# Moving the rotation of three query chunks and the bias rows from VectorE to GpSimd, from batch 1 on

## What is computed

```python
q = hidden_states @ w_q.T            # 16 heads of 32
k, v = jnp.split(hidden_states @ w_kv.T, 2, axis=-1)
def apply_rotary(t, pos, scale):
    return t * jnp.cos(pos) * scale + rotate_half(t) * jnp.sin(pos) * scale
q = apply_rotary(q, pos, xscale)
k = apply_rotary(k, pos, 1.0 / xscale)
attn = softmax(where(causal, -inf, q @ k.T))
out = (attn @ v) @ w_proj.T + b_proj
x = x + out + ffn(xn)
```

## Time and profile before

| | us |
|---|---|
| three runs: median (lowest, highest) | 1730.41 (1730.21, 1731.7) |
| the profiled execution | 1730.02 |
| its span, first instruction to last | 1728.2 |
| busy in the span: TensorE / VectorE / ScalarE / GpSimd | 1620.8 / 1205.5 / 1073.1 / 821.0 |

### The profile page before, as it was taken

The page is one execution under the profiler, slowest core; times in us unless marked ns, Lnnn a source line. Parts: engine busy times, 40 slices in busy tenths (PEclk is TensorE's granted clock), DMA queues, the critical chain, the costliest instruction groups (busy, mean ns, idle before and its releaser), DMA issues.

```text
span 1728.2 us, 40624 instructions
## 1 busy us (share of the span) xinstructions
PE 1620.8 (94%) x10811; PEld 1388.4 (80%) x10811; DVE 1205.5 (70%) x3669; ACT 1073.1 (62%) x2799; POOL 821.0 (48%) x669
## 2 busy tenths in 40 slices
PE   5887789999999999999999999899999999999999
PEld 5775667777777877777777777799999999999987
DVE  7779987777868777778687777355555555555567
ACT  3355565666757756757577577366666666666642
POOL 0213002434524524435344344277777877778760
PEclk9899899999999999999999999999999999999999
DMA  7953823434434334344344344599999999989794
GB/s 280 387 166 102 134 63 99 142 115 145 140 96 151 124 126 153 113 137 136 116 138 133 105 151 141 117 183 188 182 195 187 189 187 198 201 172 162 137 260 184
DMA packets 193091, 273.72 MB, mean 158 GB/s; under 512 B 37400, under 2 KB 133791, under 8 KB 190820
## 3 DMA queue, kind: packets, MB, share of 16 engines
q0 software_dynamic: 60352, 92.59, 24.8%
q1 hardware_dynamic: 77572, 113.01, 23.2%
q10 hardware_dynamic: 54944, 65.52, 12.8%
HBM read 121.83 MB, written 129.67 MB: 146 GB/s over the span
## 4 chain that ended last, share of the span: by engine, by line
PE 58%; DVE 18%; issue 10%; DMA 5%; POOL 4%; ACT 3%; DVEq 1%; SPq 1%; ACTq 0%; POOLq 0%
PE e_psH L1710 10%; PE e_psY L1721 10%; DVE m_sc L1088 5%; POOL sums L1675 4%; PE m_psO L1339 4%; PE m_psU L64 3%; PE m_psS L1292 3%; PE m_psT L1317 3%; PE m_psY L64 3%; PE m_psU L66 3%; PE m_psU L65 3%; DVE m_sc L1098 3%; PE m_psY L65 3%; PE m_psY L66 3%; PE e_psX L1695 3%
## 5 line engine op out<-in xcount | busy, mean ns | idle before, releaser
L1675 POOL DMA_INDIRECT sums<-e_y,e_where x287 | 445.9, 1554 | 153.4 <-issue 96.5
L856 POOL DMA_INDIRECT slot_rows<-m_row,slots x256 | 266.1, 1039 | 470.4 <-ACT m_sc L934 436.8
L934 ACT ACTIVATE m_sc<-m_sc,m_low 128x512 f32<-128x512 f32 (+3 forms) x512 | 283.7, 556 | 161.5 <-DVE m_low L1088 160.1
L1710 PE MATMUL e_psH<-e_xt,e_w_of 128*128 128x128 f32 x2296 | 305.1, 276 | 3.3 <-ACT e_xt L1570 3.3
L1721 PE MATMUL e_psY<-e_w,e_ht 128*128 x1148 | 295.7, 380 | 1.5 <-ACT e_ht L1581 1.5
L1088 DVE CUSTOM_DVE_ANT_0 m_sc<-m_psS,cst 128x512 f32<-128x512 f32 (+3 forms) x512 | 229.4, 485 | 83.1 <-PE m_psS L1292 82.5
L1710 PEld LDWEIGHTS e_psH<-e_xt,e_w_of 128*128 128x128 f32 x2296 | 280.5, 193 | 3.7 <-ACT e_xt L1570 3.5
L1576 ACT ACTIVATE e_w_of<-e_w 128x512 f32 x287 | 180.9, 630 | 118.1 <-issue 116.1
L1721 PEld LDWEIGHTS e_psY<-e_w,e_ht 128*128 128x128 f32 x1148 | 196.2, 191 | 17.2 <-issue 2.5
L1292 PE MATMUL m_psS<-m_ks,m_qs 96*128 96x256 f32 (+2 forms) x512 | 160.2, 372 | 52.1 <-DVE m_low L1088 45.1
L1631 DVE TENSOR_SCALAR e_where<-e_row,e_shifts 128x1 uint32<-128x1 uint32 x287 | 61.5, 214 | 196.5 <-DMA sums<-e_y,e_where 178.2
(11 more groups left out here) (233 smaller groups left out, 3228.2 us busy)
## 6 DMA issues: line engine op xcount, KB each, us to landing
e_row<-slot_rows ACTq DMA_DIRECT2D x287, 144.5 KB, 3.7
m_qs<-m_qhi SPq DMA_DIRECT2D x256, 64.0 KB
e_w<-in_w SPq DMA_DIRECT2D x256, 64.0 KB
f_xt<-in_x SPq DMA_DIRECT2D x8, 1024.0 KB, 11.4
m_qs<-m_qlo SPq DMA_DIRECT2D x128, 64.0 KB
m_res<-in_x SPq DMA_DIRECT2D x8, 1024.0 KB, 5.8
sums<-empty POOLq DMA_DIRECT2D x32, 256.0 KB
partial<-m_res ACTq DMA_DIRECT2D x16, 512.0 KB
```

The lines of the kernel that those rows point to most:

```text
L856: pool.indirect_dma_start(out=xs, out_offset=bass.IndirectOffsetOnAxis(ap=slots_sb[:, g, k:k + 1], axis=0), in_=row[g % 2][:, :], in_offse ...
L934: nc.scalar.activation(cols, cols, ACT.Exp, bias=low[:, h % 2, i:i + 1], scale=-1.0, accum_out=total[:, h % 2, i:i + 1]).then_inc(exp_done, 1)
L1675: pool.indirect_dma_start(out=both_sums, out_offset=bass.IndirectOffsetOnAxis(ap=where[u % NY][:, 0:1], axis=0), in_=y[u % NY][:, :], in_o ...
L1710: mm = pe.matmul(psH[u % 2][:, k * P:(k + 1) * P], w1_of[u % 2][:, c * INTER + k * P:c * INTER + (k + 1) * P], xt[u % 2][:, c * P:(c + 1) ...
```

## The change

From batch 1 on, GpSimd makes the two products and the sum of the chunks 1 to 3 and adds the four bias rows; batch 0, chunk 0 and the keys stay as they are. VectorE keeps the shuffle. The GpSimd work stands in program order among its scatters: a chunk's turn after the last scatter that waits for no more than the first row of exponentials of step 1, 5 or 9, and the bias rows after the last one that waits for no more than all rows of step 5. The core of the diff:

```diff
+            def turn_queries(b, n):
+                cos, sin = tables["q"]
+                k = QK_AT[f"q{n}"]
+                pool.wait_ge(rot_step, at(b, 3 * NQK, 3 * k + 1))
+                pool.sem_inc(pool_passed, 1)
+                nc.gpsimd.tensor_tensor(rot[:, :], rot[:, :], sin, ALU.mult).then_inc(rot_step, 1)
+                nc.gpsimd.tensor_tensor(q[:, :], q[:, :], cos, ALU.mult).then_inc(rot_step, 1)
+                pool.wait_ge(rot_step, at(b, 3 * NQK, 3 * k + 3))
+                nc.gpsimd.tensor_tensor(q[:, :], q[:, :], rot[:, :], ALU.add).then_inc(rotated, 1)
+
+            def add_bias(b):
+                pool.wait_ge(res_in, b * 16 + 16)
+                pool.wait_ge(bp_in, 16)
+                pool.sem_inc(pool_passed, 1)
+                for i in range(TB):
+                    nc.gpsimd.tensor_tensor(res[:, i, :], res[:, i, :], bp[:, :], ALU.add).then_inc(res_made, 1)
+
+            def beside(done, due):
+
+                for b in range(1, B):
+                    for n in range(1, KC):
+                        if done <= b * NH * TB + (q_slot(n) + 1) * TB + 1 < due:
+                            turn_queries(b, n)
+                        if n == 2 and done <= b * NH * TB + (q_slot(n) + 2) * TB < due:
+                            add_bias(b)
+
+            def paced(g, k):
+                return NH * TB + (g * TOPK + k) * PACE // (2 * TOPK)
+
             def scatter(g, k):
+                beside(paced(g, k - 1) if g or k else 0, paced(g, k))
...
-                if 0 in parts:
+                if 0 in parts or not parts:
...
                     nc.vector.stream_shuffle(r_, x_, [(i + HD // 2) % HD for i in range(HD)]).then_inc(rot_step, 1)
+                if 0 in parts:
...
-                        rotate(b, f"q{Q_AT[s - 1]}", (0,))
+                        rotate(b, f"q{Q_AT[s - 1]}", (0,) if first else ())
...
-                    if s - 2 in Q_AT:
+                    if first and s - 2 in Q_AT:
                         rotate(b, f"q{Q_AT[s - 2]}", (1,))
...
-                    if 5 <= s < 5 + TB:
+                    if first and 5 <= s < 5 + TB:
                         add_bias(b, s - 5)
```

More of the change, by code:

```diff
@@ L878, in pool_program @@
                 fill(g)
+            beside(paced(G - 1, TOPK - 1), B * NH * TB + NH * TB)
             for u in range(2):
```

## The result

The changed kernel took **1779.68 us** (median of 4 runs, 1778.05 to 1784.06) against 1731.06 us before: ratio 1.0287, 95% interval 1.0273 to 1.0301. It is 49 us slower, where 16 us were forecast. Its profiled execution has a span of 1776.1 us, 47.9 more than before.

What follows compares the result with a forecast made beforehand. The last-ending chain was 58% TensorE and 18% VectorE, with VectorE's extra work on the path in slots 2, 6 and 10. 1730.0 - 18.8 gained + 35.7 lost = 1746.9 us; forecast 1734 to 1762 (0.64), range 1718 to 1763.

Steps and rivals of the forecast that it cites:

- the term of slot 6: Slot 6: GpSimd's four bias rows meet VectorE's square, subtractions and scale; three hits taken, 2.6 us a batch lost.
- the high end: Slots 1, 5, 9 and 6 at their largest losses, 2.55 + 1.1 + 1.4 + 3.4 = 8.45 us a batch; 1770 us.
- Slot 1: Slot 1: GpSimd's second product and sum run beside VectorE's scale; two hits, 1.7 us a batch lost.
- Slots 5 and 9: Slots 5 and 9: the turn's hits mostly covered by TensorE; 0.4 us a batch lost in each.
- The gain: Slots 1, 2, 6, 7 and 10: VectorE work removed from the path; 2.68 us a batch, 18.8 over seven.
- more cannot go: Slots 2 and 10: savings stop at 0.34 and 0.35 us, as the 0.84 us wait for ScalarE comes back.
- the row that I chose: Batch 0 trace: the square beside a GpSimd operation took 0.43 us, so no hit in slot 6; sum stays at 1747.
- Its 1753: Slot 6: by the skill's port rule the square is held up too, a fourth hit; sum 1753 us.
- GpSimd costs nothing: Rival 1: GpSimd's operations fall beside mask operations and in VectorE's waits; 1711 us at best; chance 0.18.
- a wash: Rival 2: hits as many as the gain has, the low end; about 1729 us, no change; chance 0.09.
- The third: Rival 3: GpSimd falls behind, ScalarE's qhi and turned-score copies wait; 1770 us and more; 0.09 with high end beyond 1762.
- The prediction's last doubt: Bias rows: forecast fails in size if GpSimd's scatters push them to where VectorE waits for TensorE.

Runs made afterwards that it cites:

- the run without GpSimd's work: The changed kernel without GpSimd's products, sums and bias rows in batches 1 to 7, waits and semaphores kept; 1720.38 us, ratio 0.9929.
- the fills run: The kernel before, with GpSimd filling two spare tiles with zeros after the last exponential of slot 6 in batches 1 to 7; 1735.37 us, 1.0023.
- the run with the earlier start: Turn on VectorE as before; GpSimd's four bias rows in slot 8, a scatter or two earlier, waiting for its first mask; 1745.47 us, 1.0088.

## Why the prediction was wrong

- **Direction and mechanism: right in kind.** VectorE's scales and subtractions wait for GpSimd's additions; masks keep their length; the order in itself cost nothing (the run without GpSimd's work). The price was indeed larger than the gain.
- **The step that failed is the term of slot 6**, "three hits of 0.85, 2.6 us". It took the pairs of the earlier trace rows, which met a scale group for 2 x 0.85 us more, as two operations that each delay VectorE by a part of their length, and counted hits. Measured against the run without GpSimd's work, slot 6 costs 4.5 us a batch (26.7 + 4.8 over seven): in six of seven batches one VectorE operation waits for all the rows that are queued, 5.61 us in batch 1. The earlier trace rows could not show that: there too one operation waits to the end of GpSimd's (1.40 us at 154.20), but the engines alternate, one wait for each, as in batch 4 of the changed kernel. A bound from the same rows was at hand, though: four rows of about 1.3 us in a line can hold VectorE for some 5 us, and the high end took 3.4.
- **A term that was missing: the clock.** The prediction took 0.64 off slot 7. Without GpSimd's work slot 7 does lose 0.6. With it, four of seven batches ran slot 7 at about half the clock, and over the seven it grew by 3.1 us: 1.0 us a batch against the run without. The window of those batches before has no dip, so nothing in it priced one.
- **Slot 1: right in size.** 1.7 us were taken, (10.5 + 1.7) / 7 = 1.74 measured. That is partly luck: single scales lost from 0.4 to 1.5 us to the products and about 1.0 to the sum, and not 0.85 each. Slots 5 and 9 cost 0.7 each and not 0.4, inside the bounds given.
- **The gain: 1.4 us a batch (9.8 / 7), 1.7 in the five slots named, and not 2.68.** Slots 6 and 7 gave 0.7 and 0.6 of 0.95 and 0.64, but slots 2 and 10 under 0.1 each and not 0.35, since ScalarE's copy to qhi closes them; "more cannot go" named ScalarE's exponentials and missed what ScalarE has queued behind them. Slot 1 gave 0.24 of 0.4.
- **In sum:** 8.8 us lost a batch instead of 5.1, and 1.4 gained instead of 2.68; 7 x (8.8 - 1.4) = 52 us from batch 1 on, where 17 were forecast. Of these 35 us slot 6 makes 13, the gain 9, the clock in slot 7 makes 7 and slots 5 and 9 make 4.
- **The rule of the Trainium skill** (SBUF — State Buffer, "Who interferes with whom"), one pair of ports that one of VectorE and GpSimd holds while the other waits, was nearer than the row that I chose: the square, which reads one tile twice, waited 2.20 us for two additions. Its 1753 was short too, since I added one hit of 0.85. The section speaks of a hold for one whole instruction; 5.61 us across four rows is longer than that.
- **The rivals.** "GpSimd costs nothing" and "a wash" fell. The third's number, 1770 and more, came out, but not by its way: no wait of VectorE or ScalarE in the list of waits names GpSimd, and GpSimd's order alone cost nothing. The prediction's last doubt, that bias rows pushed to a place where VectorE waits for TensorE would cost less, was right, but less is not nothing: in slot 8 the rows on GpSimd came out 14.5 to 16 us below the same rows in slots 5 and 6, and still 20 us above the same rows on VectorE. In the changed kernel itself they did not fall there.

## What to carry to other kernels

An elementwise operation with two tiles as inputs, moved from VectorE to GpSimd, is not taken off VectorE: price it, as an upper bound, at GpSimd's full duration (here 1.28 us for what VectorE does in 0.64), summed over all that GpSimd has queued without a wait, and take off only the time that VectorE meanwhile spends waiting or on what was not held up here (masks out of PSUM, the reciprocal). Measured here, the price was 8.8 us a batch for 16.6 us of GpSimd work (13 x 1.28). Before work is moved to another engine, look for the idle time of the engine that it is on: four rows in VectorE's own idle 2.4 us brought 8.6 us, three quarters of the 11.5 that the run without GpSimd's work did. And a slot that another engine sets is cover only behind the operation which that engine waits for.

## What was not expected of the hardware

- One VectorE operation can wait for a whole run of GpSimd additions: 5.61 us in the changed kernel, and one scale, at most 0.5 us by itself, lasted 5.87 us beside four rows. It does not always: with the rows beside the masks of slot 8 the engines alternated in seven of seven batches. A gap of 0.08 us between two GpSimd operations, in which GpSimd waits for a semaphore, is enough for one VectorE operation to pass.
- An addition whose two inputs are the same tile takes GpSimd 1.05 us at 128x512, one with two tiles 1.25 to 1.3. The first holds VectorE up just the same; a fill of the same size, 0.54 us, leaves the square and the subtraction alone, and for the scale it is open.
- In a slot in which TensorE waited for 2 to 5 us, or in the next one, the granted clock often fell to its lower level, 1.2 GHz. It also fell in slot 7 of the fills run, behind slots 6 that were only 0.34 and 0.84 us longer than before. A dip cost 1.1 to 2.2 us in slot 7 of the changed kernel (4.8 against 5.95 to 7.04) and 1.5 us in slot 8 of the run with the earlier start. What decides whether a wait is followed by a dip stays open: the two slots of that run, 9.81 and 11.36 us, have the same VectorE work and the same delay by GpSimd's rows, and one has the dip and the other has none.
